# A feature that is constant one: biases, key sums and the attention denominator carried inside existing matrix products

## The reference, cut to what matters

```python
xn  = layernorm(x)                                  # no gain, no offset
qkv = xn @ Wqkv + bqkv ;  q, k, v = split(qkv)
qp, kp = elu(q) + 1, elu(k) + 1
kv  = einsum('bsd,bse->bde', kp, v)                 # per batch
num = qp @ kv ;  den = qp @ sum_s(kp)
z   = layer_norm(xn + num / (den + 1e-6), g1, b1)
ffn = (silu(z @ Wg + bg) * (z @ Wu + bu)) @ Wd + bd # 682 hidden
s   = layer_norm(z + ffn, g2, b2)
g   = silu(xn @ ternary(Wt).T * scale)
out = x + s * g
```

## Time and profile before

| | |
|---|---|
| median of 3 runs | 1225.8 us (1225.75 to 1225.92) |
| span of the profiled execution, first to last instruction | 1224.8 us |
| PE busy | 1205.1 us, 98%, 7544 products |
| PEld busy | 1080.3 us, 88% |
| DVE busy | 1083.9 us, 88%, 2467 instructions |
| ACT busy | 953.9 us, 78%, of it 148.8 us in 116 table loads |
| POOL busy | 839.6 us, 69%, of it 105.4 us in 120 additions to ksum |
| granted TensorE clock, mean | 0.997 |

### The profile page before, as it was taken

The page is one execution under the profiler, slowest core; times in us unless marked ns, Lnnn a source line. Parts: engine busy times, 40 slices in busy tenths (PEclk is TensorE's granted clock), DMA queues, the critical chain, the costliest instruction groups (busy, mean ns, idle before and its releaser), DMA issues.

```text
span 1224.8 us, 24008 instructions
## 1 busy us (share of the span) xinstructions
PE 1205.1 (98%) x7544; PEld 1080.3 (88%) x7544; DVE 1083.9 (88%) x2467; ACT 953.9 (78%) x1557; POOL 839.6 (69%) x994
## 2 busy tenths in 40 slices
...
GB/s 214 71 53 87 121 105 69 87 104 122 121 87 87 87 105 121 116 105 74 87 104 120 111 107 76 71 121 121 120 83 69 95 119 104 70 70 66 74 18 35
DMA packets 137523, 115.61 MB, mean 94 GB/s; under 512 B 12339, under 2 KB 122293, under 8 KB 137398
## 3 DMA queue, kind: packets, MB, share of 16 engines
...
## 4 chain that ended last, share of the span: by engine, by line
PE 95%; DVE 2%; issue 1%; DMA 1%; ACT 1%; POOL 0%; SPq 0%; DVEq 0%; POOLq 0%
PE bank L1278 67%; PE d_bank L1278 19%; PE xk_bank L1278 8%; PE bank L1292 1%; DVE st L930 0%; DMA xa<-z_turned 0%; DMA z_turned<-xa 0%; DVE rz L1062 0%; POOL rstd L577 0%; ACT rz L703 0%; DVE rz L1148 0%; DVE xn L982 0%; DVE xa L1082 0%; SPq L452 0%; DVE xa L993 0%
## 5 line engine op out<-in xcount | busy, mean ns | idle before, releaser
L1278 PE MATMUL bank<-zT_h,wgu_h 128*128 128x512 f32 x704 | 278.4, 395 | 0.2 <-DVE rz L1062 0.2
L1278 PE MATMUL bank<-zT_l,wgu_h 128*128 128x512 f32 x704 | 278.6, 396 | 0.0
L1278 PE MATMUL bank<-zT_h,wgu_l 128*128 128x512 f32 x704 | 278.3, 395 | 0.0
L1278 PE MATMUL d_bank<-wd_h,h_h 128*128 128x256 f32 x640 | 180.6, 282 | 0.0
L1278 PE MATMUL d_bank<-wd_h,h_l 128*128 128x256 f32 x640 | 180.2, 282 | 0.0
L1278 PE MATMUL d_bank<-wd_l,h_h 128*128 128x256 f32 x640 | 180.1, 281 | 0.0
L1103 DVE SCALAR_TENSOR_TENSOR bank<-bank,hb,hs 128x512 f32<-128x512 f32 x160 | 118.2, 754 | 55.6 <-ACT hs L703 42.8
L1278 PEld LDWEIGHTS bank<-zT_l,wgu_h 128*128 128x128 f32 x704 | 132.3, 188 | 31.4
L703 ACT ACTIVATE h_h<-bank 128x512 fp32r<-128x512 f32 x160 | 95.7, 598 | 81.4 <-DVE bank L1103 81.2
L1278 PEld LDWEIGHTS bank<-zT_h,wgu_h 128*128 128x128 f32 x704 | 132.4, 188 | 25.6 <-DVE rz L1062 1.7
L1278 PEld LDWEIGHTS bank<-zT_h,wgu_l 128*128 128x128 f32 x704 | 132.9, 189 | 23.6
...
## 6 DMA issues: line engine op xcount, KB each, us to landing
...
z_turned<-xa SPq DMA_DIRECT2D x120, 128.0 KB, 3.4
...
```

What stands on the lines that cost most here:

```text
L1278: ins = eng.matmul(dst, left, right, start=first and n == 0, stop=last and n == len(pairs) - 1, **kw)
```

## The change

- x's last normalised feature is set to 1 instead of its value (memsets of `xn` and `xq` at the start; the normalisation writes 255 columns). Wqkv's rows are corrected for that: the last row is subtracted from all others and its place taken by the bias (`projection`, `setup_k_fold`, `setup_q_fold`, `setup_v_fold`; also the ternary weights). So q, k and v come out of the products with their biases.
- `k_add` goes. `k_exp` reads the bank of K, and `k_max` does bank + 1 and the maximum in one instruction. The bank of K is now freed by `k_max`.
- Row 255 of the batch sum in `xk_bank` is the sum of the keys, since that feature is 1. Wv's last column is set up so that kv's last column is the key sum. `sum_k`, `ksum`, `kv_bias` and the products with ones go. N has 256 columns, the denominator in column 255; `attn` writes 255 columns.
- b1 @ (Wg, Wu) is made as 11 columns of d_bank (`setup_bias`, 22 products of one column) in place of three rows; the way through DRAM goes.
- The tables are written in another order. On PE, K 1 stands behind N 3 instead of ahead of N 0. On ACT, k_exp 0 stands ahead of x_res and kv_high, and k_exp 1 between silu_gate 0 and h_high 0.

```diff
 TENSOR_JOBS = steps("""
-    K 0, D 4, KV 0, KV 1, D 5, K 1, N 0, N 1, N 2, N 3, G 0, U 0, G 1, U 1, G 2, B 0, U 2, Q 0, Q 1,
+    K 0, D 4, KV 0, KV 1, D 5, N 0, N 1, N 2, N 3, K 1, G 0, U 0, G 1, U 1, G 2, B 0, U 2, Q 0, Q 1,
...
 def freed(kind, g, n):
-    "TX": ("xTl", PAIRS * g + n + 1), "K": ("k1", PAIRS * g + n + 1),
+    "TX": ("xTl", PAIRS * g + n + 1), "K": ("kp", PAIRS * g + n + 1),
...
 sync engine, start:
-eng.dma_start(raw_qk[:, :, D:2 * D], rows(wqkv[:, D:2 * D])).then_inc(s_w["k"], 16)
+def projection(dst, n, name):
+    w = slice(n * D, (n + 1) * D)
+    eng.dma_start(dst[:, 0, :], wqkv[0:P, w]).then_inc(s_w[name], 16)
+    eng.dma_start(dst[0:P - 1, 1, :], wqkv[P:LAST, w]).then_inc(s_w[name], 16)
+    eng.dma_start(dst[P - 1:P, 1, :], row(bqkv[w])).then_inc(s_w[name], 16)
+eng.dma_start(last_row[:, :], wqkv[LAST:D, :].to_broadcast([P, 3 * D])).then_inc(s_w["last"], 16)
+projection(raw_qk[:, :, D:2 * D], 1, "k")
...
 gpsimd:
-def sum_k(g, t):
-    ...
+def setup_q_fold():
+    for c, rows_ in ((0, P), (1, P - 1)):
+        part = raw_qk[0:rows_, c, 0:D]
+        eng.tensor_tensor(part, part, last_row[0:rows_, 0:D], ALU.subtract).then_inc(S["w_qf"], 1)
...
 def k_exp(g, p):
-    eng.wait_ge(S["k1"], n + 1)
+    eng.wait_ge(S["K"], n + 1)
     if n >= KU:
         eng.wait_ge(S["kp"], n - KU + 1)
-    act(part, kp[:, n % KP, :, :], ACT.Relu, "mK", scale=-1.0, bias=ones[:, 0:1])
+    act(part, job_bank("K", g, p)[:, :].rearrange("p (t n) -> p t n", t=2), ACT.Relu, "mK", scale=-1.0)
...
-def k_add(g, p):
-    ...
 def k_max(g, p):
     eng.wait_ge(S["eK"], n + 1)
-    eng.tensor_tensor(kp[:, n % KP, :, :], kp[:, n % KP, :, :], ku[:, n % KU, :, :],
-                      ALU.max).then_inc(S["kp"], 1)
+    eng.scalar_tensor_tensor(out=kp[:, n % KP, :, :],
+                             in0=job_bank("K", g, p)[:, :].rearrange("p (t n) -> p t n", t=2),
+                             scalar=1.0, in1=ku[:, n % KU, :, :], op0=ALU.add, op1=ALU.max)\
+       .then_inc(S["kp"], 1)
...
-def kv_bias(g, c):
-    ...
 def KV(g, c, dst):
-    eng.wait_ge(S["ks"], TILES * (g + GPB))
...
-    products(dst[:, D:KVW], [(ksum[:, batch % 2, w], one_zero[:, :])], "KV")
 def N(g, t, dst):
-    products(dst[:, 0:KVW], [
+    products(dst[:, 0:D], [
...
-def bias_row(n):
-    products(d_bank[n % 2][0:1, 0:w.stop - w.start],
-             [(b1c[:, k:k + 1], raw_all[:, k, w]) for k in range(DC)], "w_b1w")
+def setup_bias():
+    for n in range(2 * HF + 1):
+        w = slice(n * P, (n + 1) * P)
+        products(d_bank[0][:, n:n + 1], [(raw_all[:, k, w], b1c[:, k:k + 1]) for k in range(DC)],
+                 "w_b1w" if n == 2 * HF else None)
```

More of the change, by code:

```diff
@@ L98 @@
 VECTOR_STEPS = steps("""
[L99 to L103, removed]
+    xk_low 0, zT_low 0, zT_low 1, kv_low 0, kv_low 1, ffn_rows 0, ffn_rows 1, k_max 0, last_stats 0,
+    attn 0, last_shift 0, attn 1, attn 2, attn 3, h_rows 0, k_max 1, h_low 0, h_rows 1, a_stats 0,
+    h_low 1, q_aggregate 0, h_rows 2, a_norm 0, x_turn 0, attn_norm 0, h_low 2, k_low 0, q_elu 0,
+    z_turn 0, q_elu 1, q_low 0, k_low 1, h_rows 3, h_rows 4, q_low 1, h_low 3, x_low 0, h_rows 5,
+    x_low 1, h_low 4, h_low 5""")
 GPSIMD_STEPS = steps("""
-    xn_low 0, last_rstd 0, last_gain 0, z_g1 0, last_offset 0, xn_low 1, sum_k 0, last_gate 0,
+    xn_low 0, last_rstd 0, last_gain 0, z_g1 0, last_offset 0, xn_low 1, last_gate 0,
     last_add 0, last_gain 1, a_rstd 0, last_offset 1, q_rstd 0, last_gate 1, last_gain 2, last_gain 3,
     last_offset 2, last_gate 2, z_g1 1, last_add 1, last_add 2, last_offset 3, last_gate 3, z_g1 2,
-    z_g1 3, sum_k 1, last_add 3, sum_k 2, tail_again 0, tail_again 1, sum_k 3""")
+    z_g1 3, last_add 3, tail_again 0, tail_again 1""")
 END_JOBS = steps("""
@@ L144 @@
 FILL_VECTOR = fill("""
[L145 to L153, removed]
+    a_stats 0 0, a_stats 0 1, a_norm 0 0, a_norm 0 1, setup_k_fold 0 0, setup_k_low 0 0, xT_low 0 0, a_stats 1 0,
+    a_norm 1 0, xT_low 0 1, setup_q_low 0 0, xT_low 1 0, k_max 0 0,
+    a_stats 2 0, k_max 0 1, a_norm 2 0, xT_low 1 1, q_elu 0 0, k_max 1 0,
+    q_low 0 0, setup_gu_low_0 0 0, xT_low 2 0, k_max 1 1, a_stats 3 0, xT_low 2 1,
+    a_norm 3 0, setup_gu_low_1 0 0, q_elu 0 1, k_max 2 0, xT_low 3 0, a_stats 4 0, k_max 2 1,
+    setup_v_low 0 0, q_low 0 1, xT_low 3 1, a_norm 4 0, setup_d_bias 0 0, k_max 3 0,
+    a_stats 5 0, k_max 3 1, xT_low 4 0, setup_ternary 0 0, q_elu 1 0, xk_low 0 0, xT_low 4 1,
+    a_norm 5 0, kv_low 0 0, kv_low 0 1, x_turn 5 0, k_max 4 0,
+    attn 0 0, k_low 4 0, k_max 4 1, setup_ternary_parts 0 0, attn 0 1, attn 0 2, attn 0 3,
     q_aggregate 0 0, k_low 4 1, attn_norm 0 0, setup_d_tail 0 0, x_low 5 0, q_elu 1 1,
@@ L196, in schedule @@
     return jobs
-VECTORS = 7
+VECTORS = 5
+ROW_LOADS = 3
 HIDDEN_VECTORS = 8
@@ L1055, in attn @@
                 eng.wait_ge(S["N"], n + 1)
-                eng.tensor_scalar(den[:, n % 2, 0:1], num[:, D:D + 1], ATTN_EPS, None, ALU.add)\
+                eng.tensor_scalar(den[:, n % 2, 0:1], num[:, LAST:D], ATTN_EPS, None, ALU.add)\
                    .then_inc(S["d1"], 1)
```

209 lines of the change are left out of this document (84 added, 125 removed).

## The result

The changed kernel takes **1273.3 us** (median of 4 runs, 1271.2 to 1278.0) against 1225.8: ratio 1.039, 95% interval 1.038 to 1.041. Its profiled execution has a span of 1271.8 us, 47.0 more than before. The forecast was 1267, range 1241 to 1282.

The account below looks back on a forecast made before the run. PE, busy throughout the steady part, was taken to set the pace. From the profiled 1224.8 us, +29.4 ordinary, +13.8 batch, -0.8 iteration 27, -1 fill gave 1266.2, with 1.0 outside the span 1267 us; range 1241 to 1282.

Parts of the forecast that it names:

- likeliest case: Whole kernel: the forecast of 1267 us itself, given 70%, with its own range 1255 to 1280 us.
- First wait (G 0): Ordinary iteration: PE waits 0.5 us before G 0, which takes N 0's bank, until attn 0's addition ends.
- Second wait (G 2): Ordinary iteration: PE waits 0.95 us before G 2 for k_max 1 to free K 1's bank; G 2 1.4 us later.
- Ordinary iterations: 21 ordinary iterations with K, each 1.4 us longer (bounds 0.5 and 1.9): 29.4 us.
- N's saving "is eaten": Ordinary iteration: N's 0.05 to 0.09 us less work gains nothing, since neither wait's chain starts from N.
- Batch iterations: Six iterations with KV and K, each 2.3 us longer (bounds 1.3 and 3): 13.8 us.
- N 0's wait: Batch iteration: PE, without K 1 as cover, waits 1.9 us before N 0 for kv_low.
- Iteration 27 and the end: The seventh batch iteration, without K: still waits for kv_low, but saves 0.8 us in all.
- The table switch: ACT: each table load takes 1.28 us without drain; the rival of a longer switch, 1335 us, had 2%.
- The fill: Start of the kernel: later key weights against less work on DVE and PE, -1 us, range -4 to +3.
- Gains and waits cancel: Rival, 2%: one wait of 0.2 us an iteration, 1226 us.
- No waits, faster: Rival, 8%: k_max 1 and attn 0 come early enough, PE stays full, only its smaller work counts: 1218 us.

Follow-up runs that it names:

- e2: The changed kernel with Relu in the place of Exp in k_exp, so two table loads per iteration instead of six: 1251.3 us.
- e6: The changed kernel with k_add and the old order back, 127-row loads split, query fold later on POOL, bias products in three lots: 1215.8 us.
- e7: The kernel before with K 1 moved behind N 3 on PE and k_add 1 behind attn 3 on DVE: 1241.0 us.
- e1: The changed kernel with each DMA of 127 weight rows split into one of 112 rows and one of 15: 1264.2 us.
- e4: The changed kernel with k_add and the old order back, 127-row loads split, and the query fold behind a_rstd 1 0 on POOL: 1223.4 us.
- e9: The changed kernel, k_add still missing, with 127-row loads split, query fold behind a_rstd 1 0 and bias products in three lots: 1258.5 us.

## Why the prediction was right, and where it was wrong

The time came out within 7 us, inside the likeliest case's own range. That is partly luck: the steady part was 12 us too high and the fill 19 us too low.

**First wait (G 0): right in size, with one wrong reason.** Forecast 0.5, put down to attn 0's addition; 0.44 measured at line 1034, and the length of K and N around it as forecast. But the prediction says that the removed k_add 0 gives nothing, since ffn_rows waits for D 5. Before, ffn_rows started at 295.81, 0.57 us behind the end of D 5, because DVE was still in zT_low, behind k_add 0:

```profile
294.70 1.19 DVE L1093 TENSOR_TENSOR zT_l<-xa,zT_h 128x512 fp32r<-128x512 f32 x1
```

The 0.49 us by which the sum has attn 0 earlier come from k_add 0's absence, and they came true: ffn_rows now starts 0.67 us behind the start of D 5, before 1.22.

**Second wait (G 2): mechanism right, size too large.** Forecast 0.95; 0.45 listed as idle, 0.75 in the period by e2. The step that failed is the chain "in full": I took silu_gate 0's 0.69, Relu 0.74, load 1.30, Exp 0.63, k_max 0.74 and the way to PE 0.14 one after another, 4.24 us from silu_gate 0's start. The rows give 406.79 - 402.89 = 3.90. What is shorter: the Relu starts 0.10 before silu_gate's end, it takes 0.59 from the bank and without a bias tile instead of 0.72 from SBUF with one, k_max takes 0.69, and from its end to PE are 0.05. G 2 stands 11.50 us behind D 5; before it was 10.46. That is 1.04 for a forecast of 1.4, and the period grew by 1.02.

**Ordinary iterations: 21 x 1.02 = 21.4 us instead of 29.4.** The sentence that N's saving "is eaten" holds for this kernel. The waits cost 1.26 us against e6's 36.13, and PE's smaller and quicker work gives 0.25 of it back. With KV an iteration takes 39.94 instead of the 40.6 forecast.

**Batch iterations: 1.6 us each instead of 2.3.** Four iterations of a batch grew by 4.66 us; less three ordinary ones at 1.02, 1.60 is left. N 0's wait was placed rightly: from K 0's end (its Relu, which waited for it, starts at 354.04) to N 0 are 4.8 us, forecast 5.0. N 2 started 0.19 us late and its first product was 0.10 slower: 0.29 for a forecast of 0.35, though no wait is listed. From N 0 to G 2 were 10.6 us instead of the 11.0 forecast, the same shorter chain as above. e7 shows the cover that K 1 gave as its own mechanism, 7.7 us in six new waits.

**Iteration 27 and the end: right.** From the D 5 of iteration 26 to the last D 5 the kernel gained 0.9 us, forecast 0.8. The table switch of 1.28 us without a drain was right too (404.09 + 1.28 = 405.37, Exp at 405.38), which puts the 2.66 us of the Trainium skill's page "ScalarE: Activation LUTs" (section "What ACT_TABLE_LOAD costs") aside here as well. ACT's busy time rose by 55 us instead of 69, mostly since 128 Relus became shorter: those of the keys from 716 to 591 ns in the mean, those of the queries from 673 to 586. The queries' Relu read a bank before too and lost only its bias tile. DVE's busy time fell by 62 us instead of about 40: k_add is 43.5 of it, and k_max, the queries' maximum (which lost its bias as well) and the low parts of keys, queries and z took less.

**The fill: the step that failed.** I took -1 with bounds -4 and +3, and it was +17.7. I costed the three DMAs by the landing time of a whole one and gave 1.5 us for issue. Missed were: (1) the DMA of 127 rows, which has no like in the rows of before, and which held SP's queue for 4.6 and 5.6 us (8.9 us of the first G, e1); PE stood still longer and its clock was lower too, 0.77 in the mean of the first 30 us where it was 0.94 before and is 0.89 in e1; (2) 44 one-column products in one lot, where before there were three short jobs, and a clock at half around their end (7.1 us of the first G, e4 to e6); (3) three waits for k_max in the fill, 3.0 us listed and about 0.8 of the first G (e6 to e9), where the sum had "two k_add" less as a gain. POOL's fold ahead of the statistics of the next group waited 14.7 us for its weights and passed the lateness of the DMA on, but with the DMA split it was in nobody's way (e1). The bounds were drawn from what the change takes away, with nothing for a DMA shape and a job that the trace did not show. That POOL "loses sum_k: nothing" was true of the steady part and hid that POOL gains a step in the fill.

**The sum.** By the terms: ordinary 21.4 for 29.4, batch 9.6 for 13.8, end -0.9 for -0.8, fill +17.7 for -1. The measured terms sum to 47.8, against 47.0 by the two spans, the forecast's to 41.4.

**The rivals.** "Gains and waits cancel" came true for e4, not for this kernel. "No waits, faster" at 1218 is e6's case: with k_add kept there are no waits, and PE's smaller work counts in full, at 1215.8, some 2.4 us of it from the quicker products that no term of the sum had.
